# A recurrence's quotient from ScalarE's exp(-ln) and a Newton step on VectorE, in place of VectorE's reciprocal

## What is computed

```python
def step(carry, kv_t):
    p, q, o = carry
    kt, vt = kv_t
    no = jnp.maximum(o, u + kt)
    A = jnp.exp(o - no)
    E = jnp.exp(u + kt - no)
    y = (A * p + E * vt) / (A * q + E)
    ...
x = x + jnp.tanh(g_xattn[1]) * _L1_xattn_ref(...)   # y for the layer-normed x as k, the context as v
```

## Time and profile before

| | |
|---|---|
| median of 3 runs | 3387.77 us (3387.43 to 3389.38) |
| profiled execution, its own time | 3388.9 us |
| its span | 3387.1 us |
| TensorE busy | 2922.5 us (86%) |
| VectorE busy | 2494.4 us (74%) |
| ScalarE busy | 1724.4 us (51%) |
| GpSimd busy | 921.8 us (27%) |
| mean granted clock of TensorE | 0.95 of full speed |

### The profile page before, as it was taken

The page is one execution under the profiler, slowest core; times in us unless marked ns, Lnnn a source line. Parts: engine busy times, 40 slices in busy tenths (PEclk is TensorE's granted clock), DMA queues, the critical chain, the costliest instruction groups (busy, mean ns, idle before and its releaser), DMA issues.

```text
span 3387.1 us, 49017 instructions
## 1 busy us (share of the span) xinstructions
PE 2922.5 (86%) x18354; PEld 1703.4 (50%) x18354; DVE 2494.4 (74%) x4562; ACT 1724.4 (51%) x2661; POOL 921.8 (27%) x1361
## 2 busy tenths in 40 slices
PE   7899998892788888768888667999999999988998
PEld 3344666661444444456666433545555455544665
DVE  6787589988766667688888768777777777766333
ACT  3222344444355555179998864444445444454443
POOL 4554000001300000046776774222222222211000
PEclk9999999995999999889999878999999999999999
DMA  6422212121110102100000021000000000021000
GB/s 235 139 91 84 59 55 64 55 63 70 41 32 23 26 17 72 43 31 1 1 1 1 28 92 39 7 1 7 1 7 7 1 7 7 1 72 32 13 19 19
DMA packets 52651, 132.62 MB, mean 39 GB/s; under 512 B 6416, under 2 KB 19536, under 8 KB 51152
## 3 DMA queue, kind: packets, MB, share of 16 engines
q1 hardware_dynamic: 43216, 96.11, 9.0%
q10 hardware_dynamic: 9216, 33.56, 3.3%
HBM read 119.03 MB, written 4.19 MB: 36 GB/s over the span
## 4 chain that ended last, share of the span: by engine, by line
PE 49%; DVE 24%; issue 12%; ACT 9%; POOL 4%; DMA 1%; SPq 0%; DVEq 0%; ACTq 0%; POOLq 0%
PE psum L1263 10%; PE psum L652 6%; PE psum L2231 5%; PE psum L2761 3%; PE psum L2720 3%; ACT area_g L2306 3%; PE psum L823 3%; PE psum L2112 2%; PE psum L2745 2%; PE psum L2730 2%; PE psum L2252 2%; DVE area_a L1870 2%; PE psum L1518 2%; PE psum L1499 2%; DVE xn L3018 1%
## 5 line engine op out<-in xcount | busy, mean ns | idle before, releaser
L2306 ACT ACTIVATE area_g<-area_a 128x2048 bf16<-128x2048 f32 x168 | 334.8, 1997 | 31.4 <-POOL area_a L2175 22.2
L2231 PE MATMUL psum<-area_c,ident_bf 128*128 128x128 bf16 x3328 | 234.2, 236 | 94.1 <-DVE area_c L2340 94.1
L652 PE MATMUL psum<-area_b,area_g 128*128 128x512 f32 x640 | 284.8, 600 | 6.4 <-DVE x_stream L547 3.6
L169 POOL TENSOR_TENSOR rstd<-mean_var,eps_col 128x2 f32<-128x2 f32 x57 | 19.2, 336 | 980.7 <-DVE mean_var L747 497.1
L2231 PEld LDWEIGHTS psum<-area_c,ident_bf 128*128 128x128 bf16 x3328 | 219.1, 107 | 119.9 <-DVE area_c L2340 112.7
L2720 PE MATMUL psum<-area_b,stage 128*128 128x512 f32 (+1 forms) x512 | 237.9, 547 | 0.0
L823 PE MATMUL psum<-xT_high,area_a 128*128 128x256 f16 x1024 | 234.7, 278 | 1.4 <-DVE xT_low L762 1.4
L823 PE MATMUL psum<-xT_low,area_a 128*128 128x256 f16 x1024 | 234.3, 278 | 0.0
L2872 ACT ACTIVATE xn<-psum,small 128x384 f32<-128x384 f32 (+1 forms) x256 | 163.5, 639 | 96.0 <-DVE small L3011 95.8
L3011 DVE TENSOR_REDUCE small<-psum 128x1 f32<-128x384 f32 (+1 forms) x256 | 158.0, 617 | 72.2 <-PE psum L2721 70.4
L2637 POOL TENSOR_TENSOR small<-small,half_pow 128x4 f32<-128x4 f32 x96 | 131.7, 1372 | 273.8 <-DVE small L2958 273.8
(11 more groups left out here) (423 smaller groups left out, 7493.3 us busy)
## 6 DMA issues: line engine op xcount, KB each, us to landing
stage<-in_w ACTq DMA_DIRECT2D x24, 512.0 KB, 4.3
stage<-in_w SPq DMA_DIRECT2D x24, 512.0 KB, 3.7
area_g<-in_toeplitz SPq DMA_DIRECT2D x32, 256.0 KB, 2.6
area_b<-in_ctxT SPq DMA_DIRECT2D x15, 512.0 KB, 3.9
area_b<-area_b SPq DMA_DIRECT2D x24, 256.0 KB, 3.7
stage<-in_ctxT SPq DMA_DIRECT2D x9, 512.0 KB, 3.9
x_stream<-in_x SPq DMA_DIRECT2D x4, 1024.0 KB, 12.2
area_c<-in_ctxT SPq DMA_DIRECT2D x4, 1024.0 KB, 11.2
```

The costliest lines, as they stand in the source:

```text
L652: last = nc.tensor.matmul(psum[:, bank + m, :], toep[:, h % 2, (m - k) * P:(m - k + 1) * P], kv[:, h % 2, k, :], start=(k == 0), stop=(k = ...
L2231: last = nc.tensor.matmul(psum[:, 1, t_ * P:(t_ + 1) * P], identb[:, :], above5[:, t_, c * P:(c + 1) * P], start=(c == 0), stop=(c == KE - 1))
L2306: nc.scalar.activation(junk5[t_], z5[b % 3][:, t_, :], ACT.Sign, bias=fine5[:, par, t_:t_ + 1], scale=-1.0, accum_out=signs5[:, t_:t_ + 1] ...
```

## The change

The two reciprocals of a quotient go. ScalarE makes a first inverse y0 of the denominator d as exp(-ln d) into `wk_y` (`first_inverse`), in two instructions of 1024 elements, the second waiting for the first. VectorE then makes d y0 and n y0 (`refine`), and `ratio` makes (d y0 - 2) (n y0), which is the quotient after one Newton step with the sign turned; `add_y` takes the gate times -1, made once at the start of the stage (`S1("away1")`). ScalarE's pair stands in round c + 2 at j = 3, behind the partial sum of that step and ahead of Tanh of step 4; for batch 6 in the tail, behind the last Exp of batch 7 and ahead of `squares34`; for batch 7 behind `squares34` and ahead of `ffn_high` of the next front. `refine` stands where `invert(c, 1)` stood, at j = 6; in the tail it stands at the place of the second `invert`. Nothing stands at j = 3 on VectorE any more. The signal of the first inverse uses a semaphore of stage 0 again, from the value that it has reached there (`KD * HC`).

```diff
--- before.py
+++ after.py
@@ -125,6 +125,16 @@
             if name not in sems:
                 sems[name] = sem(name)
             return sems[name]
+
+        REUSED = {"wkv_inverted": ("kv_ready", KD * HC)}
+
+        def reused(name):
+
+            return sig(REUSED[name][0])
+
+        def after(name, n):
+
+            return sig(REUSED[name][0]), REUSED[name][1] + n
 
         def at(i, par, per, k):
 
@@ -899,6 +909,16 @@
                 act.wait_ge(sig("wkv_relu_done"), 4 * c + 2)
                 nc.scalar.activation(wk_d[:, 2:4], wk_d[:, 2:4], ACT.Exp, scale=-1.0).then_inc(sig("wkv_exp_ready"), 1)
 
+            def first_inverse(c):
+                if c < 0:
+                    return
+                act.wait_ge(sig("wkv_den_ready"), 2 * c + 1)
+                if c:
+                    act.wait_ge(sig("wkv_yT_ready"), TT * c)
+                nc.scalar.activation(wk_y, wk_den, ACT.Ln).then_inc(reused("wkv_inverted"), 1)
+                act.wait_ge(*after("wkv_inverted", 2 * c + 1))
+                nc.scalar.activation(wk_y, wk_y, ACT.Exp, scale=-1.0).then_inc(reused("wkv_inverted"), 1)
+
             def present_relu(c):
                 if c < 0:
                     return
@@ -935,6 +955,8 @@
                         sum_later(act, 5 * b + (1, 2, 3, 5, 6).index(j))
                     if j in (4, 6) and b + 1 < B:
                         ffn_high(act, front_of_ffn(b + 1), (b + 1) % 2, j // 2 - 2)
+                    if j == 3:
+                        first_inverse(b - 2)
                     if j == 6:
                         history_relu(b - 1)
                     if j == 7:
@@ -948,7 +970,9 @@
             history_exp(B - 1)
             present_relu(B - 1)
             present_exp(B - 1)
+            first_inverse(B - 2)
             squares34(act)
+            first_inverse(B - 1)
             act.wait_ge(sig("mask4_loaded"), 16)
             act.wait_ge(sig("wkv_eps_ready"), 2 * KD * B)
             for t_ in range(TT):
@@ -971,6 +995,7 @@
                 if c in (4, 5):
                     ffn_low(dve, c - 3, 0, c - 4)
             dve.wait_ge(sig("conv_added"), NTILES)
+            dc.step(nc.vector.tensor_scalar(S1("away1"), gates[:, 1:2], -1.0, None, ALU.mult))
             for z, v in ((wk_o, -1e38), (wk_p, 0.0), (wk_q, 0.0)):
                 dc.step(nc.vector.memset(z[:, :, 0:1], v))
 
@@ -992,25 +1017,27 @@
                 dve.wait_ge(sig("wkv_ev_ready"), 2 * c + 2)
                 nc.vector.tensor_tensor(wk_num, wk_num, wk_ev, ALU.add).then_inc(sig("wkv_den_ready"), 1)
 
-            def invert(c, half):
+            def refine(c):
                 if c < 0:
                     return
+                dve.wait_ge(*after("wkv_inverted", 2 * c + 2))
                 dve.wait_ge(sig("wkv_den_ready"), 2 * c + 2)
-                part_ = wk_den[:, 2 * half:2 * half + 2, :]
-                dc.step(nc.vector.reciprocal(part_, part_))
+                dc.step(nc.vector.tensor_tensor(wk_den, wk_den, wk_y, ALU.mult))
+                dc.step(nc.vector.tensor_tensor(wk_num, wk_num, wk_y, ALU.mult))
 
             def ratio(c):
                 if c < 0:
                     return
                 dc.settle()
-                nc.vector.tensor_tensor(wk_y, wk_num, wk_den, ALU.mult).then_inc(sig("wkv_y_ready"), 1)
+                nc.vector.scalar_tensor_tensor(out=wk_y, in0=wk_den, scalar=2.0, in1=wk_num, op0=ALU.subtract,
+                                               op1=ALU.mult).then_inc(sig("wkv_y_ready"), 1)
 
             def add_y(c, t_):
                 if c < 0:
                     return
                 xt = X[:, c * TT + t_, :]
                 dve.wait_ge(sig("wkv_yT_ready"), c * TT + t_ + 1)
-                nc.vector.scalar_tensor_tensor(out=xt, in0=psum[:, 1, :], scalar=gates[:, 1:2], in1=xt,
+                nc.vector.scalar_tensor_tensor(out=xt, in0=psum[:, 1, :], scalar=S1("away1"), in1=xt,
                                                op0=ALU.mult, op1=ALU.add).then_inc(sig("wkv_added"), 1)
 
             def running_max(c):
@@ -1068,14 +1095,12 @@
                         products(b - 2)
                     if j == 2:
                         totals(b - 2)
-                    if j == 3:
-                        invert(b - 2, 0)
                     if j == 4:
                         running_max(b - 1)
                     if j in (5, 7) and b + 1 < B:
                         ffn_low(dve, (b + 1) * TT + (j - 5) // 2 + 1, (b + 1) % 2, (j - 5) // 2)
                     if j == 6:
-                        invert(b - 2, 1)
+                        refine(b - 2)
                     if j == 7:
                         ratio(b - 2)
                     dve.wait_ge(sig("hid_high_ready"), n + 1)
@@ -1112,8 +1137,7 @@
             running_max(c)
             differences(c)
             scale34(dve, dc)
-            invert(c - 1, 0)
-            invert(c - 1, 1)
+            refine(c - 1)
             ratio(c - 1)
             dve.wait_ge(sig("wkv_added"), TT + TT * (c - 1))
             norm_sums(dve, dc, NEXT, 0)
@@ -1128,9 +1152,8 @@
             products(c)
             totals(c)
             squares_to_pool(dve, dc)
-            invert(c, 0)
             scales34(dve, dc)
-            invert(c, 1)
+            refine(c)
             ratio(c)
             for t_ in range(TT):
                 ffn_low(dve, 2 * TT * B + t_ + 1, 0, t_)
```

## The result

The changed kernel takes 3401.78 us (median of 6 runs, 3395.02 to 3405.04) beside 3387.60 us for the kernel before (6 runs, 3386.98 to 3389.57): a ratio of 1.0038, with an interval of 1.0027 to 1.0049. It is slower, by 14.2 us where 10.3 were forecast.

The account below looks back on a forecast made before the run. A few steps, not VectorE's total, were taken to bound each round. Rounds (+5.54 us) and tail (+4.79) summed to +10.3, so the median would be 3398.1 us, range 3391 to 3414.

Parts of the forecast that it names:

- What bounds the kernel: Rounds: a few steps bound, not VectorE's total; first reciprocal half costs 1.48 us of its 3.34, the second nothing.
- Two loads at the row's price: ScalarE's pair: one table load before Ln, one before Exp, 1.28 us each; as the forecast case, chance 0.60.
- F: Time the Ln and Exp pair holds ScalarE, loads included: taken as 4.70 us; the sum turns at 3.41.
- Rival 2: ScalarE's table switch dearer by up to 1.28 us each through pipeline stalls: F = 7.2, 3418 us; chance 0.12.
- Rival 4: Exp shares Ln's table, sparing tail loads: 3394.3 us; or the tail's load runs before the wait: 3396.8; chance 0.10.
- Ordinary rounds: Rounds 3 to 6: the pair delays Tanh of step 4; each round changes by F - 4.21 = +0.49 us.
- Round 2: Round without addition of y, its step 4 sooner: changes by F - 3.55 = +1.15 us.
- round 7: Round without a next front: changes by F - 2.27 = +2.43 us.
- the rounds' term: Rounds 2 to 7 together: 6F - 22.66 = +5.54 us.
- Tail: After round 7: batch 6's quotient 4.11 us late, the end 2F - 4.61 = +4.79 us, passed whole to stage 3.
- The sum: Rounds and tail together: 8F - 27.27 = +10.3 us, giving a median of 3398.1 us.
- rival 5: Remainder: TensorE's clock moves at the new gaps, or tail partly hidden later; a few us either way; chance 0.08.

Follow-up runs that it names:

- d: Changed kernel with Relu in place of Ln, so no table loads in the pair (logarithm left out): 3382.92 us beside 3389.47 before, ratio 0.9985.
- f: Changed kernel with ScalarE's pair moved behind Tanh of step 4 for batches 0 to 5, tail keeping the reciprocals: 3382.72 us beside 3389.62 before, ratio 0.9978.
- b: Kernel before with the new quotient only for batches 6 and 7, in the tail: 3394.25 us beside 3389.47 before, ratio 1.0020.
- a_again: The changed kernel once more, no edit: 3399.53 us beside 3389.47 before, ratio 1.0031.
- e: Changed kernel plus eight unread TensorE products ahead of the last down projection in rounds 1 to 7: 3403.57 us beside 3389.62 before, ratio 1.0039.
- g: As f, plus the new quotient for batch 7 with its pair between the front's two copies and mask rows earlier: 3384.07 us beside 3389.62 before.
- j: As g, with GpSimd's bias addition moved behind the last quotient: 3379.99 us beside 3389.78 before, ratio 0.9968.
- c: Kernel before with the new quotient only for batches 0 to 5, in the rounds: 3396.30 us beside 3389.47 before, ratio 1.0028.
- h: Changed kernel with the four mask rows ahead of ScalarE's pair for batch 7: 3401.98 us beside 3389.62 before, ratio 1.0036.

## Why the prediction was right, and what it missed

**What bounds the kernel.** Right. The first half of the reciprocal cost 1.48 us a round and not 3.34: d and f each get 1.48 back in a middle round. The second half, free by the prediction, gave nothing back.

**Two loads at the row's price.** Right: 16 loads of 1283 ns, one before each Ln and one before each Exp, and F = 4.64 where 4.70 was taken. The 0.06 is the overlap of neighbours (Tanh starts at 644.67, Exp ends at 644.77), which the sum had left out. Rival 2, a dearer switch, fell: an activation starts 0.01 us after its load and the load 0.02 us after the activation ahead. By the Trainium skill (ScalarE: Activation LUTs, "What ACT_TABLE_LOAD costs") the load's 1283 ns agree with these rows, and its 2.66 us for a switch with the drain is not borne out here: load and gaps are 1.3. Rival 4 fell too, since Exp didn't stay in Ln's table but had a load of its own behind each Ln. The section "Table sets: the hidden batching unit" of that page of the Trainium skill lists a set with both; by these rows it wasn't chosen here.

**Ordinary rounds.** Right in each term. L1087 of step 4 was to come 8.53 us after step 3's and comes 8.46; step 5 was to follow at 4.32 and follows at 4.25, the wait for TensorE gone. A round changes by +0.35 where F - 4.21 was +0.49, for the 0.06 of F and another 0.07 of the same overlaps. **Round 2** is +1.01 for +1.15, **round 7** +2.28 for +2.43: the rounds' term is +4.7 and was +5.54.

**Tail.** Right. VectorE waits 8.28 us for Exp; the quotient of c = 6 is 4.17 us late for 4.11, the second low half +4.85 for +4.79, and it waits for the copy behind the mask rows (3.69). VectorE's own side was later than forecast, 828.9 for 828.3 at the first low half, counted as before (839.86 less the 10.97 us by which the tail began later), because its scales had grown; the forecast had not looked at them, and it cost nothing only because ScalarE was later still. b shows the term alone at +4.9 in the stretch and 3394.25 - 3389.47 = +4.8 in the time: nothing later gives it back.

**The sum.** By its own terms it measures +4.7 and +4.85, +9.6 for +10.3. The time moved by +14.2 in the first comparison and +10.1 in a_again. The second lies on the forecast by chance, since its stretch is longer by 12.1. What the sum lacks in the stretch is the clock: rival 5 named it and left it at "a few us either way", without a sign. The place to find most of it was in view. The prediction said that rounds 3 to 6 use up the 1.34 us wait of VectorE for TensorE at step 5, that is, TensorE is ahead from there on, and did not ask where TensorE then waits. It waits at the last down projection of the round, 3.4 us in place of 1.5 in rounds 2 to 6, and in some rounds the clock falls in that wait: 3.6 us of loss in the profile of after, 1.1 in that of a_again. e shows that filling the wait takes this away inside the stretch; that it is worth anything in the time of the kernel isn't shown. The rest, 0.79 us in after and 1.48 in a_again, has no such wait ahead of it, and losses of 0.8 us like the first stand also in d, f, g and j, which wait 1.5 to 1.6 us at that place. What must come together for the clock to fall stays open: round 3 in c has the same wait and no loss, as rounds 2, 3, 5 and 6 in a_again.

**Size of the measurement.** The two comparisons of the same kernel differ by 4 us in their medians, 14.2 and 10.1 over before; with clock terms of 4.4 and 2.5 in their profiled stretches and a rest that varies by some us from execution to execution, no more than "10 to 14" can be said. The sum's own terms are shown by the stretches; that the difference between 10 and 14 in the times is the clock is not, since e has +14.0 in its time, and +9.8 in its profiled execution, which is without these losses.

## What to carry to other kernels

Moving work off a busy engine is worth what the steps show where that engine is waited for, here 1.48 us of 6.56, and it costs what the queue of the other engine holds up. The same pair, two tables and all, was 8 us slower or 6 faster in the stretch by standing ahead of Tanh or behind it: first look for the place where nobody waits, then count the work. And where a change makes an engine idle longer in every round, ask of TensorE what its clock does behind that idle time.

## What was not expected of the hardware

- A table load is 1283 ns, 16 times of 16, with 0.01 to 0.02 us on each side and no further gap. Ahead of a wait on a semaphore it can also run early: 6.5 us before its Ln in h (824.35 against 830.85), 2.4 us in g; in the changed kernel the same load ran only behind the wait (831.05).
- VectorE's scales of one element took 1.15 and 1.23 us in place of 0.14 while GpSimd worked through its additions of 128 x 512 (two of them, 2.48 us). With these moved away they took 0.15. The reciprocal of 128 x 512 that ran beside the same additions in the kernel before took 3.35 us, as elsewhere.
- The granted clock fell to half in waits of 3.4 us in one round and stayed up through the same wait in another, with the same instructions ahead. The kernel before has low stretches too, at the start of most rounds, and they cost nothing. In d, f, g, h, j and the first profile of after, such a stretch was some 7 us long in place of 3 in one or two rounds, and the step from 1 to 2 was 0.8 us longer.
- What follows the stretch took 2549.0 to 2562.8 us over twelve profiles with the same instructions: a difference of 10 us between two single spans says nothing of an edit, the stretch does.
